# Graph network on one core: two buffers for the edge term, bias transfers inside the setup loop, and 38 source gathers there instead of 44

## The reference, cut to what matters

```python
e = ea @ We
alpha = h @ a_s
alpha = alpha[src] + (h @ a_d)[dst] + e @ a_e        # e @ a_e is the edge term
alpha = leaky_relu(alpha, NEG_SLOPE)
alpha = _segment_softmax(alpha, dst, N)
out = segment_sum(h[src] * alpha[:, None], dst, num_segments=N) + b
```

## Time and profile before

| | us |
|---|---|
| median of 3 runs | 2042.78 (2036.03 to 2043.71) |
| profiled execution | 2044.88 |
| its span | 2042.8 |
| setup 1 | 0 to 48.2 |
| setup 2 | 48.2 to 164.6 |
| first dense block | 164.6 to 510.9 |
| busy over the span: PE, DVE, ACT, POOL | 75%, 80%, 76%, 53% |
| mean granted TensorE clock | 0.878 |

### The profile page before, as it was taken

How to read it: one execution, slowest core, us unless ns; L and a number is a source line. 1 busy time by engine, 2 the same in 40 slices (tenths; PEclk the granted TensorE clock), 3 DMA queues, 4 the chain that set the end, 5 groups by cost and what they waited for, 6 DMA issues and landing times. The chain is left out here.

```text
span 2042.8 us, 40093 instructions
## 1 busy us (share of the span) xinstructions
PE 1536.4 (75%) x9041; PEld 1123.4 (55%) x9041; DVE 1630.1 (80%) x8491; ACT 1545.9 (76%) x7842; POOL 1089.7 (53%) x919
## 2 busy tenths in 40 slices
PE   3764888886788877885978884978875978875940
PEld 2433555553677764544975544975544975543830
DVE  5775999996899967986877986877986877986940
ACT  0674999996799967993987983988983978973730
POOL 0876787750455538772008771018771018772777
PEclk9996999998799977995997996988996988996975
DMA  8753233321321122213231213231213231214421
GB/s 165 194 145 91 73 100 97 97 72 37 92 67 55 55 71 65 60 41 85 66 101 39 61 45 79 68 109 33 61 41 90 67 107 25 61 45 119 110 53 34
DMA packets 134375, 157.14 MB, mean 77 GB/s; under 512 B 58714, under 2 KB 91879, under 8 KB 134137
## 3 DMA queue, kind: packets, MB, share of 16 engines
q1 hardware_dynamic: 77545, 128.36, 22.6%
q0 software_dynamic: 56160, 25.44, 6.0%
q10 hardware_dynamic: 432, 0.79, 0.1%
HBM read 106.25 MB, written 68.36 MB: 85 GB/s over the span
## 5 line engine op out<-in xcount | busy, mean ns | idle before, releaser
L222 POOL DMA_INDIRECT S<-row_t,rowI x400 | 537.9, 1345 | 562.0 <-DMA row_t<-T 422.4
L938 PE MATMUL bank<-AC,XT 128*125 128x390 f32 x800 | 327.9, 516 | 0.3
L1007 ACT ACTIVATE R<-bank 125x128 f32<-125x128 f32 x1200 | 322.8, 306 | 0.0
L1007 ACT ACTIVATION_READ_ACCUMULATOR R<-bank 125x1 f32 x1200 | 279.7, 240 | 0.0
L210 PE MATMUL bank<-ident,Y 125*128 125x125 f32 x800 | 131.2, 290 | 118.0 <-ACT Y L958 59.2
L1870 PE MATMUL bank<-WCX,XT 128*125 128x130 f32 (+1 forms) x1400 | 218.7, 279 | 0.1
L210 PEld LDWEIGHTS bank<-ident,Y 125*128 125x128 f32 x800 | 97.9, 150 | 218.3 <-issue 140.7
L222 POOL DMA_INDIRECT S<-in_x,srcI x100 | 157.9, 1579 | 99.7 <-issue 99.7
L1051 DVE BATCH_NORM_STATS2 st<-R 125x6 f32<-125x128 f32 x800 | 173.2, 279 | 31.0 <-issue 30.6
L1870 PEld LDWEIGHTS bank<-WCX,XT 128*125 128x125 f32 x1400 | 182.6, 189 | 6.7 <-ACT XT L1907 0.4
L918 PEld LDWEIGHTS bank<-AC,XT 128*125 128x125 f32 x800 | 105.6, 204 | 114.2 <-ACT SB L1024 112.6
(11 more groups left out here) (447 smaller groups left out, 4755.1 us busy)
## 6 DMA issues: line engine op xcount, KB each, us to landing
row_t<-T SPq DMA_DIRECT2D x40, 573.1 KB
R<-in_x SPq DMA_DIRECT2D x100, 224.0 KB
out_rows<-R SPq DMA_DIRECT2D x100, 224.0 KB
R<-m_t SPq DMA_DIRECT2D x25, 546.9 KB
S<-row_t,rowI POOLq DMA_INDIRECT x400
T<-in_edge_attr SPq DMA_DIRECT2D x5, 1120.0 KB
x_t<-XB SPq DMA_DIRECT2D x50, 112.0 KB
R<-x_t SPq DMA_DIRECT2D x25, 224.0 KB
```

Source lines behind the costliest of these rows:

```text
L222: pool.indirect_dma_start(to, None, table, bass.IndirectOffsetOnAxis(ap=idx, axis=0), bounds_check=rows - 1, oob_is_err=False).then_inc(do ...
L938: nc.tensor.matmul(LAYERS[a][0:P, 0:3 * D + 6], h0(g, a), ACB[:, 0:3 * D + 6], start=True, stop=True).then_inc(layers_done.s, 1)
L1007: ins = nc.scalar.activation(JUNK[:, a * 3 + l, :], LAYERS[a][0:P, l * D:(l + 1) * D], ACT.Square, scale=D ** -0.5, accum_out=NRM[:, g % N ...
```

## The change

The edge term gets a second buffer (columns 6300 to 6800 of the large buffer R, beside the old one in AL) and two semaphores, one for even groups and one for odd, so that the copy of term g waits for the store of term g-2. The table VT moves from column 6700 to 10900, since the new buffer covers its old place. The sixteen bias transfers are issued one a turn in the turns 2 to 17 of SP's loop, after that turn's loads. SOON falls from 44 to 38, so that six gathers move from setup 2 to the first dense block, which then has 163.

```diff
-SOON = 44
+SOON = 38
-        VT = RB[0:C, 6700:6700 + D]
+        VT = RB[0:C, 10900:10900 + D]
-        s_aet = sem("edge_term_transposed")
+        s_aet = [sem("edge_term_placed_even"), sem("edge_term_placed_odd")]
-        AES = AL[0:L, :, :].rearrange("l a e -> l (a e)")
+        AES = [AL[0:L, :, :].rearrange("l a e -> l (a e)"), RB[0:L, 6300:6300 + Q * P]]
                 def keep_edge_term(g):
                     dve.wait_ge(s_aep, g + 1)
-                    if g:
-                        dve.wait_ge(s_aet, 16 * g)
-                    nc.vector.tensor_copy(AES, PT[2 + g % 2][0:L, 0:Q * P]).then_inc(s_aes, 1)
+                    if g >= 2:
+                        dve.wait_ge(s_aet[g % 2], 16 * (g // 2))
+                    nc.vector.tensor_copy(AES[g % 2], PT[2 + g % 2][0:L, 0:Q * P]).then_inc(s_aes, 1)
...
+                def place_bias(a, j):
+                    if a == 0 and j == 0:
+                        sp.wait_ge(s_e4, 1)
+                        sp.wait_ge(s_ebz, 1)
+                    k = j * Q + a if j < 3 else KS - 1
+                    sp.dma_start(EB[k:k + 1, a * D:(a + 1) * D], E4[(j + 1) % L:(j + 1) % L + 1, :]).then_inc(s_eb, 16)
...
                 def place_edge_term(g):
                     sp.wait_ge(s_aes, g + 1)
-                    sp.dma_start(term_t[:, g * Q * P:(g + 1) * Q * P], AES).then_inc(s_aet, 16)
+                    sp.dma_start(term_t[:, g * Q * P:(g + 1) * Q * P], AES[g % 2]).then_inc(s_aet[g % 2], 16)
...
                     dma2(sp, TGTB[g % 4], dst_v[g * Q * P:(g + 1) * Q * P].unsqueeze(0).broadcast_to([P, Q * P]),
                          dst_rows[g % 4].s)
+                    if 2 <= g < 18:
+                        place_bias((g - 2) // Q, (g - 2) % Q)
                     if g > 5 and g % 5 == 3:
                         keep_masks(g // 5 - 1)
...
-                sp.wait_ge(s_e4, 1)
-                sp.wait_ge(s_ebz, 1)
-                for a in range(Q):
-                    for j in range(3):
-                        sp.dma_start(EB[j * Q + a:j * Q + a + 1, a * D:(a + 1) * D],
-                                     E4[j + 1:j + 2, :]).then_inc(s_eb, 16)
-                    sp.dma_start(EB[KS - 1:KS, a * D:(a + 1) * D], E4[0:1, :]).then_inc(s_eb, 16)
                 sp.wait_ge(s_eb, 16 * 4 * Q)
-                sp.wait_ge(s_aet, 16 * EG)
+                sp.wait_ge(s_aet[0], 16 * (EG - EG // 2))
+                sp.wait_ge(s_aet[1], 16 * (EG // 2))
```

More of the change, by code:

```diff
@@ L1338, in _ @@
                     load_masks(sp)
-                    sp.dma_start(AE[:, :, :], term_t.rearrange("l (t e) -> t l e", t=C)).then_inc(s_aet, 16)
+                    sp.dma_start(AE[:, :, :], term_t.rearrange("l (t e) -> t l e", t=C)).then_inc(s_aet[0], 16)
                     for n in range(NU):
@@ L1345, in _ @@
                             dma2(sp, row_v[:, 2 * (n + 1 - STORE):2 * n + 2, :], T[:, 2 * (n + 1 - STORE):2 * n + 2, :], s_rows)
-                    sp.wait_ge(s_aet, 16 * EG + 16)
+                    sp.wait_ge(s_aet[0], 16 * (EG - EG // 2) + 16)
                     sp.wait_ge(*x_stage.at(10))
```

## The result

The changed kernel takes 2019.43 us in the median of four runs (2018.1 to 2023.81), the kernel before 2041.83 in the same set of runs; the ratio is 0.9899 with a 95% interval of 0.9873 to 0.9924, a gain of 20.6 us (15.5 to 25.9), or 22.4 us between the two medians. The forecast was 2017 us and a gain of 26. The profiled execution is the slowest of the first four, 2023.81 us, its span 2021.7.

The account below looks back on a forecast made before the run. Waits, not a full engine, bound the second setup block. DVE and SP would end at 136.6 us, POOL at 138.5, the later instead of 164.6: 26 us off the 2042.78 median gives 2017 us, range 2008 to 2028.

Parts of the forecast that it names:

- The waits: Setup 2's loop: DVE's 18.8 us of waits for the previous term's store fall to 1.0, at most 4.8.
- under 3: Sign of being right: L683's waits for the edge term's store total under 3 us.
- B: Rival: a denser DMA queue keeps stores late in setup 2's loop; 2024 us, or 2032 if all waits return; chance 0.09.
- C: Rival: L683 waits for the product, so two buffers change nothing; only the tail is won, 2032 us; chance 0.02.
- The bias transfers at nothing: Sixteen bias issues leave setup 2's 10.1 us tail and cost nothing in SP's loop, covered by its waits for DVE.
- D: Rival: bias issues block SP in setup 2's loop, the block ends 37 us later, 2080 us; chance 0.02.
- none after 120: Sign of being right: no bias transfer is issued after 120 us in setup 2.
- DVE's and SP's end: Setup 2: the path of DVE's loop and SP's tail ends at 136.6 us instead of 164.6.
- The gathers: Setup 2: POOL's 38 gathers, delayed 27.1 us by DVE's turns, end at 137.9 us.
- Rival A: Gathers slow with DVE's unbroken busy time, so GpSimd ends setup 2 at 145; gain 19, 2023 us; chance 0.17.
- the step to the next block (some 0.6 us): End of setup 2: the next block starts some 0.6 us behind POOL's last gather, at 138.5 us.
- The rest shifted as it stands: All stages after setup 2 keep their lengths; six more gathers cost the first dense block nothing, with 60 us left.

Follow-up runs that it names:

- e5: The changed kernel itself, unaltered, run again in a second set of runs; ratio 0.9878 to the kernel before, median 2016.66 us.
- e1: The changed kernel with only the two buffers: 44 gathers, bias transfers behind the loop as before; ratio 0.9938 to the kernel before.
- e2: The changed kernel with only the bias transfers moved into the loop: one buffer used, 44 gathers; ratio 0.9960 to the kernel before.
- e7: The changed kernel with 34 gathers in the setup instead of 38; ratio 0.9846 to the kernel before, median 2011.65 us.
- e3: The changed kernel with 44 gathers in the setup instead of 38; ratio 0.9923 to the kernel before.
- e8: The changed kernel with 44 gathers and the compare of source ids done on two inputs, the bound broadcast; ratio 0.9967 to the kernel before.
- e12: The changed kernel with 44 gathers, the compare on two inputs and the small copy L692 moved from DVE to ScalarE; one run, 2032.02 us.
- e9: The changed kernel with 34 gathers and a third edge-term buffer at partitions 32 to 35 of AL; ratio 0.9877 to the kernel before.

## Why the prediction was right, point by point

*The waits.* Right in kind and nearly in size. They went from 18.8 to 3.3 us, with 1.0 forecast, 4.8 as the bound and "under 3" as the sign of being right, so that sign is missed by 0.3. All six left over are under 1 us. The other profiles with two buffers range from 1.2 to 3.4, and e5, the same program again, has 6.2 with one wait of 1.5, past the bound. Turns without a wait take 2.84 us. B and C are refuted by e1.

*The bias transfers at nothing.* Right for the changed kernel: SP still waits for DVE in its loop, no issue stands in the tail, and the longest store issue is 1.49 us beside 1.41 before, so D did not happen. The last of them is issued at 97.98, where "none after 120" was the sign. In a loop with one buffer they cost something (e2), which the prediction did not say: with one buffer there is no turn of slack for the store, which may be why; the waits that grew there are those for PE.

*DVE's and SP's end.* The sum gave 136.6. It was 136.2 (last store issued at 134.56, landed 1.4 to 1.6 us after) in the changed kernel, and e7, where nothing else ends the block, gave 135.25. The other profile of the changed kernel, e5, gives 138.6 (136.76, 0.24 and 1.6), with its 3 us more of waits.

*The gathers.* The 38th ends at 137.14 (134.8 in e5), forecast 137.9: the count by turns gives 27.1 us of delay, and the rows 26.5 (72.0 us from 65.09 to 137.14 less 29 x 1.57). Rival A, the rate of the densest stretch, is refuted as a price (145), but not in kind: POOL is what ended the block. Six gathers and the idle stretch were counted at 12.8 us; in e3 POOL's last gather ends 13.5 us later than in the changed kernel, and the block 12.1, since the step behind it is 1.4 us shorter. The rule that the prediction cites put a gather's delay down to the compare; e8, with the compare on two inputs, speaks against that.

*The step that failed* is "the step to the next block (some 0.6 us)". The runs show 4.0 us behind the last of 36 or 38 gathers, and 2.6 behind 44. Of the 4.0 us, 1.7 are the landing of the last gather, which the forecast left out although it counted the landing of the last store; the 2.3 behind it have no cause that the rows show (0.9 with 44 gathers). In the kernel before SP was last, and no row showed what a block change behind POOL costs; the row nearest to it, the 3.40 us of idle behind the 39th gather, was there, but I gave it to the 44 gathers alone. With 4.0 in place of 0.6 the forecast block end is 141.9; the profile has 141.15. The gain of 26 is mis-sized by these 3.4 us, and 22.4 between the medians is about what is left. In e5 the block ends at 138.79, close to the forecast 138.5, and the gain is 24.9, but that is luck: there the last gather ended 3.1 us earlier than forecast, DVE's and SP's path 2 us later, and the two ended the block together. The median of 2019.43 lies within 2.5 us of the forecast, and the changed kernel has the forecast's order of events: POOL last, DVE and SP just before it.

*Two small slips in the sums.* Half of the old waits put 9.4 in the place of 1.0, which gives 145.0 for B and not 146, and a gain of 29 less half the spread gives 2009.9 and not 2009. Neither changes the forecast.

*The rest shifted as it stands.* Right for the dense block: 346.6 us beside 347.4 before, from first load to first load, and POOL has 62 us left, forecast 60. The layer behind it was not constant. Its length, from its first load of masks to the first gather of the next block, was 254.0 us before and 257.3 in the profile of the changed kernel, and 250.8 to 254.1 in the profiles of e1 to e12. The two last rows of the first fence show where: in the second stretch of 26 us PE's clock is 0.73, where e5 has 1.00 and the kernel before 0.92:

```profile
510.60:536.60 26.00, 22.69 (x184) 19.93 (x184) 26.00 (x174) 26.00 (x72) 15.13 (x24) 1.00 0.18 53
```

That row is e5's, whose span is 2012.5 against 2021.7 for the same program. PE did 147 matmuls in that stretch in the one profile and 184 in the other. The layer took 257.3 and 251.7 us. So some 6 of the 9.2 us between two profiles of one program arise in that layer, together with a longer time at 1.2 GHz at its start; they are no effect of the change. That the clock is their whole cause is not shown.

## What to carry to other kernels

Edits that touch different paths of one block do not add up one by one. Alone, the buffers moved the block's end by 12.0 us and the bias transfers by 6.7; together (e3) they moved it by 11.4, since POOL ended the block. The fewer gathers alone moved nothing that can be told from chance, and added to the other two they brought 12.1 us more. In the time the three alone gave 12.7, 8.2 and 2.0 us (the last from 0.6 slower to 4.7 faster), the first two together 15.7, and all three 20.6 to 24.9. So try an edit again after each other one: what it is worth depends on which path ends the block then. Before you move the split between stages, ask for each engine not only when its last instruction ends but how long after it the next block starts; where an engine has never been last, the trace does not show that price, and the split should leave it room (34 gathers rather than 38). Count the landing of the last transfer on every queue, not on one only. A wait for a small store that recurs every turn wants a second buffer, and one is enough when the store takes less than two turns: the third (e9) took the last 2.3 us of waits away and the block ended no earlier.

## What the runs showed of the hardware that had not been expected

- A gather beside DVE's loop mostly takes exactly one turn of it, 2.54 + 0.30 = 2.84 us, or 2.74 + 0.30 with a turn of 3.05 (e8, e12); free it takes 1.27. Taking the one-input compare and the small copy out of the turn changes nothing (e12). DMA load alone does not do it (1.27 to 1.71 us at a share of 0.92).
- POOL stands still for 3.0 to 3.9 us behind every 39th gather of a series, in all runs. The next block starts 3.9 to 4.0 us behind its last gather with 36 or 38 of them, 2.6 to 2.7 with 44; 1.7 of these are the gather's own transfer. What POOL waits for in the rest is not shown.
- The delay between POOL and DVE goes both ways: a gather that started 0.03 us behind a mask (e9, 98.02) took its free 1.27 us, and DVE's compare took 0.86 us instead of 0.47. Without a gather beside it the compare is at 0.47 again. A copy from PSUM to partition 32 instead of 0 by itself cost 0.1 us before it and 0.14 in its turn (e9).
